# Four single score banks against two double banks in a self attention of a two-layer transformer kernel

## The chip, the cores and the metric

The kernel runs on one core of a Trainium2 chip. The metric is the device time of one execution in microseconds (us), as the median of several runs. Lower is better.

## What is computed

The reference applies two transformer blocks to x of 4 batches x 1024 tokens x 256 channels. Each block is a self attention, a cross attention on a context of 77 tokens and a gated feed forward, each behind a layer norm and with a residual. Block 0 has 16 heads of width 16 and quantised weights; block 1 has 16 heads of width 64. All is float32. The change touches the self attention of block 0 alone:

```python
sim = jnp.einsum('bihd,bjhd->bhij', q, k) * scale
attn = jax.nn.softmax(sim, axis=-1)
out = jnp.einsum('bhij,bjhd->bihd', attn, v).reshape(Bq, Nq, D)
return linear(out, ow, ob)
```

## The kernel before

`attend_narrow` works in 16 **steps**, four for each batch; a step takes a group of four heads. A step has 16 **slots**. The softmax subtracts each query's maximum, so the scores are computed twice: once as queries x keys to find the maximum (line 1501, "scores", reduced by VectorE in line 1369), and once as keys x queries with the maximum already folded into the matmul as extra rows (line 1518, "shifted"), from which ScalarE takes the exponential (line 1481). TensorE multiplies these by the values (line 1530). The first product runs 13 to 16 slots ahead of the second: while step i is in its slots, the maxima of step i+1 (and of the first 3 slots of step i+2) are found. Step 0's maxima, 64 reductions, and 12 of step 1 come before the first slot; at the end, from slot 13 of step 14 on, there are no scores left to do.

The order on TensorE in a slot is written out: the first pair of shifted products (sh0), the scores of key half f = 0, at some slots one **extra**, the scores of f = 1, the second pair of shifted products (sh1), the values of two slots before. A pair is two heads, r = 0 and r = 1, whose matmuls use rows 0 to 63 and 64 to 127 of the array. VectorE takes its work in the same order. TensorE executes in this order and stops at a wait, with all that stands behind it.

The extras are: "back" (slots 2 and 10, four transposes of the output, line 1539, then on VectorE lines 1391 and 1396), "rows" (slot 4 after an odd step, slot 12 of an odd step, line 1547, then ScalarE line 1464 and VectorE line 1404), "turn" (slot 13, the transpose of the maxima, line 1508, then lines 1382 and 1385; VectorE forms the negated maxima just before, line 1373), and "y" (slots 7 and 8 after each fourth step, the output projection, line 1560, then line 1415).

Scores and extras share one ring of PSUM banks, `bank`, in the order in which they come. Every entry of the ring ("unit") has a number u, lies in bank u % 4, and may be written when unit u - 4 has been released: `pe.wait_ge(s_free, u - 3)`, where s_free counts the releases (it starts at RING0 = 4). In a slot with an extra the units are f0 r0, f0 r1, extra, f1 r0, f1 r1 ("y" takes two). The shifted products have a ring of three banks of their own, `stb`, which the exponentials free (p_ready).

```python
for r in range(2):
    u = at["s", i, slot, f, r]
    rows = slice(64 * r, 64 * r + SROWS)
    pe.wait_ge(s_free, u - 3)
    t.matmul(bank[u % 4][:, :], q[cur][rows, j, qb * P:(qb + 1) * P], k_[cur][rows, j, f * HALF:(f + 1) * HALF],
             start=True, stop=True, tile_position=(64 * r, 0)).then_inc(s_ready, 1)
```

Of the kernel before, what the change touches and what calls it, by code (L numbers as in the profile page):

```python
# [5 lines left out]
F32 = mybir.dt.float32  # L6
# [90 lines left out]
class Program:  # L97
# [1125 lines left out]
    def attend_narrow(self, L, x_sb, ident, wo, bo):  # L1223
        nc = self.nc
        QB, KC, HALF, G, HD, W = N // P, N // P, N // 2, L.group, L.hd, L.tile
        SLOTS = 2 * KC
        NP, DEPTH, EARLY, RING0 = 8, 3, 3, 4
        STEPS, NG = L.steps, L.ng
        LAG = 2
        SROWS, TROWS = 3 * HD, 3 * HD + 2  # L1230
# [6 lines left out]

        def scores_of(i, slot):
            for f in range(2):
                for r in range(2):  # L1240
                    unit("s", i, slot, f, r)

        for slot in range(SLOTS):
            scores_of(0, slot)
# [3 lines left out]
        for i in range(STEPS + 1):  # L1248
            for s in range(SLOTS if i < STEPS else 10):
                n, slot = (i + 1, EARLY + s) if s < SLOTS - EARLY else (i + 2, s - SLOTS + EARLY)  # L1250
                for f in range(2):
                    if n < STEPS:
                        unit("s", n, slot, f, 0), unit("s", n, slot, f, 1)
# [12 lines left out]

        with ExitStack() as st:
# [91 lines left out]
            def _(dve):  # L1359
# [2 lines left out]

                def top(i, slot, f):
                    qb, j = slot // 2, slot % 2
                    for r in range(2):
                        u = at["s", i, slot, f, r]
                        dve.wait_ge(s_ready, u + 1)
                        c = ((r * 2 + j) * QB + qb) * 2 + f
                        v.tensor_reduce(mx[:, i % 2, c:c + 1], bank[u % 4][:, :], AX_X, ALU.max).then_inc(s_free, 1)  # L1369

                def negate(i):
                    dve.wait_ge(s_free, at["s", i, SLOTS - 1, 1, 1] + 1)
                    v.tensor_reduce(negm[:, :], mx[:, i % 2, :].rearrange("p (c f) -> p c f", f=2), AX_X, ALU.max,
                                    negate=True).then_inc(negm_done, 1)

                def turned(i):
                    u, par = at["turn", i], i % 2
                    rows = bank[u % 4][0:4 * QB, 0:P]
                    dve.wait_ge(s_ready, u + 1)
                    if i >= 2:  # L1380
                        dve.wait_ge(m_in[(i - 2) % DEPTH], ((i - 2) // DEPTH + 1) * 64)
                    v.tensor_scalar(mm[par][:, 0, :].bitcast(U32), rows.bitcast(U32), HI12, None,
                                    ALU.bitwise_and).then_inc(m_cut, 1)
                    dve.wait_ge(m_cut, i + 1)
                    v.tensor_tensor(mm[par][:, 1, :], rows, mm[par][:, 0, :], ALU.subtract).then_inc(s_free, 1)

                def normalise(n):
                    half, g, u = n % 2, n // 2 % 2, at["back", n // 2, n % 2]
                    view = bank[u % 4][:, :].rearrange("p (b h w) -> p b h w", b=4, w=W)
                    dve.wait_ge(s_ready, u + 1)  # L1390
                    v.reciprocal(rec[:, half, :, :].unsqueeze(3), view[:, :, :, HD:HD + 1]).then_inc(rec_done, 1)
                    dve.wait_ge(rec_done, n + 1)
                    if n >= 4 and g == 0:
                        dve.wait_ge(s_ready, at["rows", n // 2 - 1, half] + 1)
                    out = on[:, half, :, G * HD * g:G * HD * (g + 1)].rearrange("p b (h w) -> p b h w", w=HD)
                    v.tensor_tensor(out, view[:, :, :, 0:HD], rec[:, half, :, :].unsqueeze(3).broadcast_to((P, 4, G, HD)),
                                    ALU.mult).then_inc(s_free, 1)

                def low(n):
# [4 lines left out]
                    v.tensor_tensor(o_lo[:, ch, cols], bank[u % 4][:, :], o_hi[:, ch, cols].bitcast(F32),  # L1404
                                    ALU.subtract).then_inc(s_free, 1)

                def project(i, half):
                    b = i // NG
# [39 lines left out]
            def _(act):  # L1448
# [10 lines left out]
                def high(n):  # L1459
                    half, ch, u = n % 2, n // 4 % 2, at["rows", n // 2, n % 2]  # L1460
                    act.wait_ge(s_ready, u + 1)
                    if n // 2 >= NG:
                        act.wait_ge(s_ready, at["y", (n // 2 // NG) * NG - 1, half, 1] + 1)
                    a_.activation(o_hi[:, ch, half * HALF:(half + 1) * HALF], bank[u % 4][:, :], ACT.Copy).then_inc(hi_done, 1)

                for i in range(STEPS + 1):
                    if i == 1:
# [20 lines left out]
            def _(pe):  # L1488
# [4 lines left out]
                def score(i, slot, f):  # L1493
                    cur, qb, j = i % DEPTH, slot // 2, slot % 2
                    if slot == 0 and f == 0:
                        pe.wait_ge(q_in[cur], (i // DEPTH + 1) * QLOADS)
                    for r in range(2):
                        u = at["s", i, slot, f, r]
                        rows = slice(64 * r, 64 * r + SROWS)
                        pe.wait_ge(s_free, u - 3)  # L1500
                        t.matmul(bank[u % 4][:, :], q[cur][rows, j, qb * P:(qb + 1) * P], k_[cur][rows, j, f * HALF:(f + 1) * HALF],  # L1501
                                 start=True, stop=True, tile_position=(64 * r, 0)).then_inc(s_ready, 1)

                def turn(i):
                    u = at["turn", i]
                    pe.wait_ge(negm_done, i + 1)
                    pe.wait_ge(s_free, u - 3)
                    t.transpose(bank[u % 4][0:4 * QB, 0:P], negm[:, :], ident[:, :]).then_inc(s_ready, 1)

                def shifted(i, s, j):  # L1510
                    cur, half, c = i % DEPTH, s // KC, s % KC
# [22 lines left out]
                def back(n):  # L1534
                    half, u = n % 2, at["back", n // 2, n % 2]
                    pe.wait_ge(o_ready, n + 1)
                    pe.wait_ge(s_free, u - 3)
                    for k in range(4):
                        ins = t.transpose(bank[u % 4][:, k * P:(k + 1) * P], osb[:, half, k * P:(k + 1) * P], ident[:, :])
                    ins.then_inc(s_ready, 1)  # L1540

                def rows(n):
                    half, u = n % 2, at["rows", n // 2, n % 2]
                    pe.wait_ge(s_free, at["back", n // 2, half] + 1)
                    pe.wait_ge(s_free, u - 3)
                    for k in range(4):
                        ins = t.transpose(bank[u % 4][:, k * P:(k + 1) * P], on[:, half, k, :], ident[:, :])
                    ins.then_inc(s_ready, 1)

                def project(i, half):  # L1550
                    pe.wait_ge(s_free, at["rows", i, half] + 1)
                    pe.wait_ge(w_low, 1)
                    for j in range(2):
                        u = at["y", i, half, j]
                        pe.wait_ge(s_free, u - 3)
                        for k in range(2):
                            tok = slice((half * 4 + 2 * j + k) * P, (half * 4 + 2 * j + k + 1) * P)
                            for n, (ch, o, w) in enumerate((ch, o, w) for ch in range(DC)
                                                           for o, w in ((o_hi, w_hi), (o_hi, w_lo), (o_lo, w_hi))):
                                ins = t.matmul(bank[u % 4][:, k * D:(k + 1) * D], o[:, ch, tok], w[:, ch, :],  # L1560
                                               start=n == 0, stop=n == 3 * DC - 1)
                        ins.then_inc(s_ready, 1)

                for slot in range(SLOTS):
                    for f in range(2):
# [1871 lines left out]
```

## Time and profile before

| | |
|---|---|
| median of 3 runs | 4218.95 us (4212.62 to 4226.44) |
| span of the profiled execution, first to last instruction | 4217.9 us |
| TensorE busy over the span | 93% |
| VectorE busy | 66% |
| ScalarE busy | 44% |
| GpSimd busy | 44% |
| first score of this self attention, last value product | 180.7 us, 949 us |
| line 1369, maxima: instructions, mean | 1024, 683 ns |
| line 1481, exponentials: instructions, mean | 1024, 601 ns |
| line 1518, shifted products: instructions, mean | 1024, 472 ns |

PE is TensorE, PEld its weight load, DVE VectorE, ACT ScalarE, POOL GpSimd, SP the queue that issues most DMAs. Line numbers are those of the kernel. "<-" in brackets names what ended the idle time of the engine before an instruction. Matmuls overlap, and the ends of matmuls are modelled, so a busy TensorE need not be at its peak. The profiled execution's own time was not recorded beside its span; the span lies 1.05 us under the median of the three runs.

### The profile page before, as it was taken

What the parts mean: (1) busy time and instruction counts of PE and PEld (TensorE: products, weight loads), DVE (VectorE), ACT (ScalarE), POOL (GpSimd) and SP (SyncE); (2) the same over time, 40 slices, a digit from 0 to 9 for tenths busy, and PEclk for the clock granted to TensorE, in tenths of its full rate; (3) what the DMA queues carried; (4) which work ended last, traced back from release to release, by engine and by line L of the source; (5) the groups of instructions that cost most, each with busy time, mean ns of one, the idle gap of its engine ahead of it and who ended that gap; (6) DMA issues with size and microseconds to landing.
All of it is one profiled execution on the core that took longest, in us unless ns stands there. A gap on an engine that the chain in (4) does not pass through costs nothing. (4 is left out here: it accounts for less than half of the span.)

```text
span 4217.9 us, 64445 instructions
## 1 busy us (share of the span) xinstructions
PE 3909.5 (93%) x24639; PEld 2598.3 (62%) x24639; DVE 2770.9 (66%) x4547; ACT 1839.2 (44%) x2746; POOL 1859.2 (44%) x1203
## 2 busy tenths in 40 slices
PE   3799999994998997998999999999999979999899
PEld 2533443433557886884666666666666647777787
DVE  6599999953536654435676767676766737665665
ACT  1267777771443333442333333333333334444333
POOL 1288970001203002005777777877787753222200
PEclk9789999996779998997999999999999989999899
DMA  4734434405622005883211111121112010000100
GB/s 159 180 56 77 59 57 48 42 2 94 102 43 52 22 13 197 306 308 103 75 51 51 64 63 51 51 76 51 51 51 76 26 31 10 10 10 1 42 15 17
DMA packets 314421, 294.96 MB, mean 70 GB/s; under 512 B 133420, under 2 KB 237292, under 8 KB 313860
## 3 DMA queue, kind: packets, MB, share of 16 engines
q1 hardware_dynamic: 311460, 281.88, 25.7%
q0 software_dynamic: 2656, 8.97, 0.7%
q8 instruction: 197, 3.23, 0.3%
q14 instruction: 108, 0.88, 0.1%
HBM read 161.92 MB, written 127.28 MB: 69 GB/s over the span
## 5 line engine op out<-in xcount | busy, mean ns | idle before, releaser
L1741 POOL TENSOR_TENSOR f_sums<-f_sums,f_probs 128x1024 f32<-128x1024 f32 x384 | 915.5, 2384 | 154.8 <-ACT f_probs L1860 117.1
L1860 ACT ACTIVATE f_probs<-f_st 128x1024 f32<-128x1024 f32 x512 | 525.0, 1027 | 938.7 <-PE f_st L1906 933.9
L1758 DVE TENSOR_REDUCE f_mx<-f_s 128x1 f32<-128x512 f32 x1024 | 659.8, 686 | 380.7 <-PE f_s L1883 369.4
L1369 DVE TENSOR_REDUCE f_mx<-f_s 128x1 f32<-128x512 f32 x1024 | 638.6, 683 | 50.8 <-PE f_s L1501 28.4
L1481 ACT ACTIVATE f_probs<-f_st 128x512 f32<-128x512 f32 x1024 | 535.9, 601 | 225.6 <-PE f_st L1518 225.5
L1883 PE MATMUL f_s<-f_k,f_q 64*128 64x512 f32 x3072 | 515.0, 415 | 18.6 <-DMA f_k<-k 12.5
L1906 PE MATMUL f_st<-f_q,f_k 64*128 64x512 f32 x3072 | 485.2, 390 | 1.1 <-ACT f_probs L1860 1.0
L1920 PE MATMUL f_acc<-f_probs,f_v 128*64 128x512 f32 x2048 | 465.0, 596 | 0.0
L1883 PEld LDWEIGHTS f_s<-f_k,f_q 64*128 64x128 f32 x3072 | 341.2, 189 | 166.6 <-issue 112.1
L1906 PEld LDWEIGHTS f_st<-f_q,f_k 64*128 64x128 f32 x3072 | 366.4, 184 | 25.9 <-ACT f_probs L1860 3.8
L1518 PE MATMUL f_st<-f_q,f_k 50*128 50x512 f32 x1024 | 332.7, 472 | 6.9 <-ACT f_probs L1481 6.8
L588 POOL TENSOR_TENSOR f_ve<-f_var,f_const 128x4 f32<-128x4 f32 x48 | 10.0, 209 | 695.9 <-DVE f_var L569 695.7
L1518 PEld LDWEIGHTS f_st<-f_q,f_k 50*128 50x128 f32 x1024 | 135.8, 185 | 277.5 <-ACT f_probs L1481 263.7
L1920 PEld LDWEIGHTS f_acc<-f_probs,f_v 128*64 128x64 f32 x2048 | 141.3, 137 | 265.9 <-issue 257.0
L1501 PE MATMUL f_s<-f_k,f_q 48*128 48x512 f32 x1024 | 267.3, 455 | 22.5 <-DMA f_k<-k 22.1
L1530 PE MATMUL f_acc<-f_probs,f_v 128*32 128x512 f32 x2048 | 273.0, 606 | 0.0
L1781 DVE RECIPROCAL f_rd<-f_s 128x512 f32<-128x512 f32 x64 | 214.9, 3358 | 72.3 <-PE f_s L1929 72.3
L1906 PE MATMUL f_st<-f_m,f_mones 64*128 64x512 f32 x1024 | 247.8, 389 | 0.0
L3289 ACT ACTIVATE f_gate<-f_pg,f_bias 128x512 f32<-128x512 f32 x128 | 88.0, 688 | 349.1 <-PE f_pg L3335 349.1
L765 DVE TENSOR_TENSOR f_stage<-f_pc,f_stage 128x512 f32<-128x512 f32 x160 | 110.2, 691 | 189.7 <-ACT f_stage L795 189.7
L1737 POOL TENSOR_TENSOR f_sums<-f_probs 128x1024 f32<-128x1024 f32 x64 | 153.3, 2395 | 183.9 <-ACT f_probs L1860 183.9
L3214 DVE SCALAR_TENSOR_TENSOR f_u<-f_pa,f_bias,f_gate 128x512 f32<-128x512 f32 x128 | 96.1, 751 | 202.0 <-PE f_pa L3335 201.9
(320 smaller groups left out, 7874.5 us busy)
## 6 DMA issues: line engine op xcount, KB each, us to landing
q<-f_stage SPq DMA_DIRECT2D x80, 512.0 KB, 2.9
k<-f_stage SPq DMA_DIRECT2D x80, 512.0 KB, 2.9
f_q<-q SPq DMA_DIRECT2D x32, 1024.0 KB, 5.0
f_k<-k SPq DMA_DIRECT2D x32, 1024.0 KB, 7.3
v<-f_v_stage SPq DMA_DIRECT2D x64, 256.0 KB, 3.1
f_v<-v SPq DMA_DIRECT2D x32, 512.0 KB, 8.5
f_q<-q SPq DMA_DIRECT2D x96, 128.0 KB, 4.2
f_k<-k SPq DMA_DIRECT2D x96, 128.0 KB, 6.9
```

The source lines that it names most:

```text
L1369: v.tensor_reduce(mx[:, i % 2, c:c + 1], bank[u % 4][:, :], AX_X, ALU.max).then_inc(s_free, 1)
L1481: a_.activation(probs[:, n % NP, e % 2, :], stb[k % 3][:, :], ACT.Exp, scale=L.scale).then_inc(p_ready, 1)
L1501: t.matmul(bank[u % 4][:, :], q[cur][rows, j, qb * P:(qb + 1) * P], k_[cur][rows, j, f * HALF:(f + 1) * HALF], start=True, stop=True, tile ...
L1518: t.matmul(stb[n % 3][:, :], k_[cur][rows, j, c * P:(c + 1) * P], q[cur][rows, j, half * HALF:(half + 1) * HALF], start=True, stop=True, t ...
L1530: ins = t.matmul(acc[W * h:W * h + W, :], vs[cur][:, c, h, :], p, start=c == 0, stop=c == KC - 1, tile_position=(0, W * h))
L1741: g_.tensor_tensor(out, out, probs[:, n % NP, :, :], ALU.add).then_inc(sum_done, 1)
L1758: v.tensor_reduce(mx[:, i % 2, c:c + 1], bank[u % 3][:, :], AX_X, ALU.max).then_inc(s_free, 1)
L1781: v.reciprocal(rd[:, half, :], bank[u % 3][:, :]).then_inc(s_free, 1)
L1860: a_.activation(probs[:, s % NP, :, :], stb[s % 2][:, :, :], ACT.Exp, scale=L.scale).then_inc(p_ready, 1)
L1883: ins = t.matmul(bank[u % 3][:, :], q[cur][rows, a, qb * P:(qb + 1) * P], k_[cur][rows, c, f * HALF:(f + 1) * HALF], start=r == 0, stop=r ...
L1906: ins = t.matmul(stb[s % 2][:, h, :], lhs, rhs, start=r == 0, stop=r == 3, tile_position=(64 * h, 0))
L1920: ins = t.matmul(acc[W * h:W * h + W, :], vs[cur][:, c, h, :], probs[:, s % NP, h, :], start=c == 0, stop=c == KC - 1, tile_position=(0, W ...
```

## The change

The ring becomes two banks of double size. One unit now holds both heads of a pair, its release is one count, and one VectorE instruction takes both maxima. Extras take a whole double bank each and use half of it; "y" uses both halves as one unit, with one addition of 1024 columns instead of two of 512. A unit u may be written when unit u - 2 has been released. The layout of `mx` follows.

```diff
-        NP, DEPTH, EARLY, RING0 = 8, 3, 3, 4
+        NP, DEPTH, EARLY, RING0 = 8, 3, 3, 2
...
             for f in range(2):
-                for r in range(2):
-                    unit("s", i, slot, f, r)
+                unit("s", i, slot, f)
...
-                        unit("y", i - 1, s - 7, 0), unit("y", i - 1, s - 7, 1)
+                        unit("y", i - 1, s - 7)
...
-            mx = sb("mx", [P, 2, 4 * QB * 2])
+            mx = sb("mx", [P, 2, 2, 2 * QB * 2])
...
-            bank = [ps(f"s{k}", [P, 512]) for k in range(4)]
+            bank = [ps(f"s{k}", [P, 2, 512]) for k in range(2)]
...
-                    for r in range(2):
-                        u = at["s", i, slot, f, r]
-                        dve.wait_ge(s_ready, u + 1)
-                        c = ((r * 2 + j) * QB + qb) * 2 + f
-                        v.tensor_reduce(mx[:, i % 2, c:c + 1], bank[u % 4][:, :], AX_X, ALU.max).then_inc(s_free, 1)
+                    u, c = at["s", i, slot, f], (j * QB + qb) * 2 + f
+                    dve.wait_ge(s_ready, u + 1)
+                    v.tensor_reduce(mx[:, i % 2, :, c], bank[u % 2][:, :, :], AX_X, ALU.max).then_inc(s_free, 1)
...
-                    for j in range(2):
-                        u = at["y", i, half, j]
-                        k = b * QB + half * 4 + 2 * j
-                        xt = x_sb[:, k:k + 2, :]
-                        dve.wait_ge(biased, b + 1)
-                        dve.wait_ge(s_ready, u + 1)
-                        v.tensor_tensor(xt, xt, bank[u % 4][:, :].rearrange("p (t d) -> p t d", d=D),
-                                        ALU.add).then_inc(s_free, 1)
+                    b, u = i // NG, at["y", i, half]
+                    k = b * QB + half * 4
+                    xt = x_sb[:, k:k + 4, :]
+                    dve.wait_ge(biased, b + 1)
+                    dve.wait_ge(s_ready, u + 1)
+                    v.tensor_tensor(xt, xt, bank[u % 2][:, :, :].rearrange("p j (t d) -> p (j t) d", d=D),
+                                    ALU.add).then_inc(s_free, 1)
...
+                    u = at["s", i, slot, f]
+                    pe.wait_ge(s_free, u - 1)
                     for r in range(2):
-                        u = at["s", i, slot, f, r]
                         rows = slice(64 * r, 64 * r + SROWS)
-                        pe.wait_ge(s_free, u - 3)
-                        t.matmul(bank[u % 4][:, :], q[cur][rows, j, qb * P:(qb + 1) * P], k_[cur][rows, j, f * HALF:(f + 1) * HALF],
-                                 start=True, stop=True, tile_position=(64 * r, 0)).then_inc(s_ready, 1)
+                        ins = t.matmul(bank[u % 2][:, r, :], q[cur][rows, j, qb * P:(qb + 1) * P],
+                                       k_[cur][rows, j, f * HALF:(f + 1) * HALF], start=True, stop=True, tile_position=(64 * r, 0))
+                    ins.then_inc(s_ready, 1)
```

The turn, back and rows transposes and their readers change in the same way: `bank[u % 4]` becomes `bank[u % 2]` (its first half), and `u - 3` becomes `u - 1`.

## Rows read from the trace of the kernel before

**Rows 1.** Busy time of each engine in a steady stretch of the stage; "x" counts instructions.

```profile
core 0: us, PE busy (x) PEld busy (x) DVE busy (x) ACT busy (x) POOL busy (x), PEclk, DMA share, GB/s
360.00:857.00 497.00, 492.25 (x3072) 202.62 (x3071) 467.14 (x797) 380.60 (x729) 233.04 (x93) 1.00 0.41 53
```

**Rows 2.** Timeline of one plain slot and the next one's start: start, length, instructions.

```profile
519.92 0.50 PE L1518 MATMUL f_st<-f_q,f_k 50*128 50x512 f32 x2
520.26 0.86 PE L1501 MATMUL f_s<-f_k,f_q 48*128 48x512 f32 x4
520.46 2.07 ACT L1481 ACTIVATE f_probs<-f_st 128x512 f32<-128x512 f32 x4 [0.54 <-PE f_st L1518]
520.63 0.18 PEld L1501 LDWEIGHTS f_s<-f_k,f_q 48*128 48x128 f32 x1 [0.18 <-DVE f_mx L1369]
...
521.10 0.18 PEld L1518 LDWEIGHTS f_st<-f_q,f_k 50*128 50x128 f32 x1 [0.29 <-ACT f_probs L1481]
...
521.53 1.06 PE L1530 MATMUL f_acc<-f_probs,f_v 128*32 128x512 f32 x8
...
522.53 0.50 PE L1518 MATMUL f_st<-f_q,f_k 50*128 50x512 f32 x2
```

**Rows 3.** Timeline of a slot of the last step, which has no scores.

```profile
916.30 0.73 PE L1518 MATMUL f_st<-f_q,f_k 50*128 50x512 f32 x3
916.83 2.07 ACT L1481 ACTIVATE f_probs<-f_st 128x512 f32<-128x512 f32 x4 [0.54 <-PE f_st L1518]
917.48 0.18 PEld L1518 LDWEIGHTS f_st<-f_q,f_k 50*128 50x128 f32 x1 [0.89 <-ACT f_probs L1481]
...
917.90 1.06 PE L1530 MATMUL f_acc<-f_probs,f_v 128*32 128x512 f32 x8
918.90 0.29 PEld L1518 LDWEIGHTS f_st<-f_q,f_k 50*128 50x128 f32 x3 [0.84 <-ACT f_probs L1481]
```

**Rows 4.** VectorE's opening, and reductions of 512 and of 2048 columns elsewhere.

```profile
181.52 38.36 DVE L1369 TENSOR_REDUCE f_mx<-f_s 128x1 f32<-128x512 f32 x64 [22.24 <-PE f_s L1501]
```

```profile
L288 DVE TENSOR_REDUCE f_ext<-f_w 128x1 f32<-128x512 f32 x6 | 4.1, 678 | 3.2 <-DMA f_w<-L_xattn_q_w 2.7 <-DMA f_w<-L_xattn_v_w 0.5
...
L288 DVE TENSOR_REDUCE f_ext<-f_w 128x1 f32<-128x2048 f32 x1 | 2.3, 2276 | 0.0
```

**Rows 5.** Timeline of a slot with a "back".

```profile
525.13 0.50 PE L1518 MATMUL f_st<-f_q,f_k 50*128 50x512 f32 x2
...
525.91 0.69 DVE L1369 TENSOR_REDUCE f_mx<-f_s 128x1 f32<-128x512 f32 x1
...
526.51 0.65 PE L1501 MATMUL f_s<-f_k,f_q 48*128 48x512 f32 x2
...
528.32 0.50 PE L1518 MATMUL f_st<-f_q,f_k 50*128 50x512 f32 x2
```

**Rows 6.** Timeline of a "y" slot, from its second pair of scores to the next slot.

```profile
427.20 0.49 PE L1501 MATMUL f_s<-f_k,f_q 48*128 48x512 f32 x2
...
428.86 0.50 PE L1518 MATMUL f_st<-f_q,f_k 50*128 50x512 f32 x2
```

**Rows 7.** Timeline, TensorE: start and end of a "rows" slot, and of two "turn" slots.

```profile
508.94 0.50 PE L1518 MATMUL f_st<-f_q,f_k 50*128 50x512 f32 x2
...
512.11 0.50 PE L1518 MATMUL f_st<-f_q,f_k 50*128 50x512 f32 x2
...
533.53 0.50 PE L1518 MATMUL f_st<-f_q,f_k 50*128 50x512 f32 x2
...
536.76 0.50 PE L1518 MATMUL f_st<-f_q,f_k 50*128 50x512 f32 x2
```

```profile
489.32 0.50 PE L1518 MATMUL f_st<-f_q,f_k 50*128 50x512 f32 x2
...
492.73 0.50 PE L1518 MATMUL f_st<-f_q,f_k 50*128 50x512 f32 x2
```

**Rows 8.** Two stretches around the rise of TensorE's clock (PEclk, the share granted).

```profile
210.00:220.00 10.00, 8.34 (x14) 3.74 (x14) 9.96 (x18) 0.00 (x0) 9.99 (x5) 0.50 0.00 0
236.40:240.00 3.60, 3.60 (x27) 1.68 (x23) 2.65 (x5) 2.46 (x5) 3.46 (x2) 1.00 1.77 62
```

More of the change, by code:

```diff
@@ L1252, in attend_narrow @@
                     if n < STEPS:
-                        unit("s", n, slot, f, 0), unit("s", n, slot, f, 1)
+                        unit("s", n, slot, f)
                     if f == 0 and s == SLOTS - EARLY and i + 1 < STEPS:
@@ L1364, in top @@
                     qb, j = slot // 2, slot % 2
[L1365 to L1369 removed]
+                    u, c = at["s", i, slot, f], (j * QB + qb) * 2 + f
+                    dve.wait_ge(s_ready, u + 1)
+                    v.tensor_reduce(mx[:, i % 2, :, c], bank[u % 2][:, :, :], AX_X, ALU.max).then_inc(s_free, 1)
                 def negate(i):
[L1372 to L1373 removed]
+                    dve.wait_ge(s_free, at["s", i, SLOTS - 1, 1] + 1)
+                    v.tensor_reduce(negm[:, :], mx[:, i % 2, :, :].rearrange("p r (c f) -> p (r c) f", f=2), AX_X, ALU.max,
                                     negate=True).then_inc(negm_done, 1)
@@ L1377, in turned @@
                     u, par = at["turn", i], i % 2
-                    rows = bank[u % 4][0:4 * QB, 0:P]
+                    rows = bank[u % 2][0:4 * QB, 0, 0:P]
                     dve.wait_ge(s_ready, u + 1)
@@ L1388, in normalise @@
                     half, g, u = n % 2, n // 2 % 2, at["back", n // 2, n % 2]
-                    view = bank[u % 4][:, :].rearrange("p (b h w) -> p b h w", b=4, w=W)
+                    view = bank[u % 2][:, 0, :].rearrange("p (b h w) -> p b h w", b=4, w=W)
                     dve.wait_ge(s_ready, u + 1)
@@ L1403, in low @@
                     dve.wait_ge(hi_done, k + 1)
-                    v.tensor_tensor(o_lo[:, ch, cols], bank[u % 4][:, :], o_hi[:, ch, cols].bitcast(F32),
+                    v.tensor_tensor(o_lo[:, ch, cols], bank[u % 2][:, 0, :], o_hi[:, ch, cols].bitcast(F32),
                                     ALU.subtract).then_inc(s_free, 1)
                 def project(i, half):
-                    b = i // NG
-                    for j in range(2):
-                        u = at["y", i, half, j]
-                        k = b * QB + half * 4 + 2 * j
-                        xt = x_sb[:, k:k + 2, :]
-                        dve.wait_ge(biased, b + 1)
-                        dve.wait_ge(s_ready, u + 1)
-                        v.tensor_tensor(xt, xt, bank[u % 4][:, :].rearrange("p (t d) -> p t d", d=D),
-                                        ALU.add).then_inc(s_free, 1)
+                    b, u = i // NG, at["y", i, half]
[5 more added lines that the diff above has]
+                                    ALU.add).then_inc(s_free, 1)
                 for slot in range(SLOTS):
@@ L1462, in high @@
                     if n // 2 >= NG:
-                        act.wait_ge(s_ready, at["y", (n // 2 // NG) * NG - 1, half, 1] + 1)
-                    a_.activation(o_hi[:, ch, half * HALF:(half + 1) * HALF], bank[u % 4][:, :], ACT.Copy).then_inc(hi_done, 1)
+                        act.wait_ge(s_ready, at["y", (n // 2 // NG) * NG - 1, half] + 1)
+                    a_.activation(o_hi[:, ch, half * HALF:(half + 1) * HALF], bank[u % 2][:, 0, :], ACT.Copy).then_inc(hi_done, 1)
                 for i in range(STEPS + 1):
@@ L1506, in turn @@
                     pe.wait_ge(negm_done, i + 1)
-                    pe.wait_ge(s_free, u - 3)
-                    t.transpose(bank[u % 4][0:4 * QB, 0:P], negm[:, :], ident[:, :]).then_inc(s_ready, 1)
+                    pe.wait_ge(s_free, u - 1)
+                    t.transpose(bank[u % 2][0:4 * QB, 0, 0:P], negm[:, :], ident[:, :]).then_inc(s_ready, 1)
                 def shifted(i, s, j):
@@ L1536, in back @@
                     pe.wait_ge(o_ready, n + 1)
-                    pe.wait_ge(s_free, u - 3)
+                    pe.wait_ge(s_free, u - 1)
                     for k in range(4):
-                        ins = t.transpose(bank[u % 4][:, k * P:(k + 1) * P], osb[:, half, k * P:(k + 1) * P], ident[:, :])
+                        ins = t.transpose(bank[u % 2][:, 0, k * P:(k + 1) * P], osb[:, half, k * P:(k + 1) * P], ident[:, :])
                     ins.then_inc(s_ready, 1)
@@ L1544, in rows @@
                     pe.wait_ge(s_free, at["back", n // 2, half] + 1)
-                    pe.wait_ge(s_free, u - 3)
+                    pe.wait_ge(s_free, u - 1)
                     for k in range(4):
-                        ins = t.transpose(bank[u % 4][:, k * P:(k + 1) * P], on[:, half, k, :], ident[:, :])
+                        ins = t.transpose(bank[u % 2][:, 0, k * P:(k + 1) * P], on[:, half, k, :], ident[:, :])
                     ins.then_inc(s_ready, 1)
@@ L1552, in project @@
                     pe.wait_ge(w_low, 1)
[L1553 to L1562, printed above, removed]
+                    u = at["y", i, half]
+                    pe.wait_ge(s_free, u - 1)
+                    for k in range(4):
+                        tok = slice((half * 4 + k) * P, (half * 4 + k + 1) * P)
+                        for n, (ch, o, w) in enumerate((ch, o, w) for ch in range(DC)
+                                                       for o, w in ((o_hi, w_hi), (o_hi, w_lo), (o_lo, w_hi))):
+                            ins = t.matmul(bank[u % 2][:, k // 2, k % 2 * D:(k % 2 + 1) * D], o[:, ch, tok], w[:, ch, :],
+                                           start=n == 0, stop=n == 3 * DC - 1)
+                    ins.then_inc(s_ready, 1)
                 for slot in range(SLOTS):
```

## The prediction

> **What bounds the kernel now.** The page comes first, to find the stage: the edit touches the 770 us of the first self attention and nothing behind it, so only that stretch is read. Second comes the table of busy time over a steady part of it [rows 1]: of 497 us TensorE is busy 492 and VectorE 467, or 94%. That reads as if VectorE's maxima set the pace, and the timeline of a plain slot seems to confirm it [rows 2]: TensorE's slot starts at 519.92 and the next at 522.53, 2.61 us apart, a second weight load at 520.63 waits for a maximum, and four maxima of 683 ns lie in it. Third, and against it, comes a slot of the last step [rows 3], which has no scores and so no maxima at all. It lasts from 916.30 to 918.90, 2.60 us. The slot is as long without VectorE's work as with it, so VectorE does not set it.
>
> What does is a circle between TensorE and ScalarE. The first exponential starts 0.54 after the slot; the second matmul of sh1 waits for it, since the ring of shifted products has three banks, and goes 1.18 after the slot's start, both with scores (521.10) and without (917.48); the values follow 0.43 later and hold TensorE for 1.00, and then the next slot starts: 1.18 + 0.43 + 1.00 = 2.61 [rows 2, 3]. The scores fit into TensorE's wait for ScalarE. I hold this circle for the bound of the plain slots.
>
> **The cost of the new maximum.** Before, 64 maxima in a row took 38.36 us [rows 4]. The last one's recorded length is 0.68, so they start (38.36 - 0.68) / 63 = 0.598 us apart, although each is recorded at 0.683. A reduction of 2048 columns took 2276 ns against 678 for 512, so a column costs 1598 / 1536 = 1.04 ns [rows 4], and 512 more columns 0.533 us. A maximum over both banks should thus last 0.683 + 0.533 = 1.216, and such maxima should start 0.598 + 0.533 = 1.131 apart, where two single ones took 1.196. That is 0.065 per pair. No row shows a reduction with the new pair form. The dearest bound is no saving at all: a length of 2 x 0.683 = 1.37, 0.15 more than I take. Cheaper than 1.04 ns a column no row suggests. I take 1.216, since two rows of one kind of instruction give the slope.
>
> The Trainium skill bears on this from two sides ("Perfetto Trace Analysis", section Optimizing Scalar/DVE Operations). It gives about 125 ns of overhead for each VectorE instruction on PSUM and says that larger operations help if the engine is saturated; with 512 instructions fewer that would be an estimate of 64 us gained if VectorE were the bound. In the same place it says that if VectorE isn't saturated but causes bubbles on other engines, breaking instructions up may let work complete sooner. This change does the reverse of the latter. The rows above speak for the second case.
>
> **Plain slots: nothing.** Pair f0 would be ready when its first half is now, and VectorE starts it 0.78 after the slot's start (525.91 - 525.13, where VectorE is idle too) [rows 5]. Two pairs take 2 x 1.131 = 2.26, so the f1 pair is recorded as done at 0.78 + 1.131 + 1.216 = 3.13, which is 0.52 after the next slot's start. The f1 scores there start around 0.6 now, and anything up to about 0.9 leaves sh1's second matmul at 1.18. What covers the change is the wait for ScalarE; were it gone, TensorE would be held by the maxima at 2.26 a slot. At the dear bound the f1 pair is done at 3.43, or 0.82 in: still covered, barely. Plain slots cost 0.
>
> **Slots with an extra: about half a microsecond each.** This is where the change bites. Before, the units of such a slot are f0 r0, f0 r1, extra, f1 r0, f1 r1; with four banks f1 r0 needs the release of a unit of the slot before, and f1 r1 that of f0 r0, which is one short maximum. Now the units are f0, extra, f1 in two banks: f1 must wait until the whole f0 pair of the same slot is reduced, since the extra has taken the other bank. It goes at 0.78 + 1.216 + 0.05 = 2.05, the 0.05 being the step from a recorded end on VectorE to the start that it releases: the f0 r0 maximum ends at 525.91 + 0.69 = 526.60, and the second matmul of the pair started there goes at 526.51 + 0.65 - 0.50 = 526.66. Before, the first of that pair went at 526.51, or 1.38 [rows 5]. Behind it on TensorE stand sh1, the values and the next slot; all engines wait for these. How far the next slot is from an f1 pair that goes late with nothing left to wait for, the "y" slot shows: 427.20 to 428.86, 1.66 us [rows 6]. So each slot with one extra becomes 2.05 + 1.66 = 3.71 long. VectorE's work on the extra falls behind f0 as before, and its f1 maximum then ends 0.1 to 0.3 into the next slot, which is early enough; nothing is given back later, because the next slot is again bound by the circle.
>
> Now the kinds, with their lengths before:
> - "back", 528.32 - 525.13 = 3.19 [rows 5]: +0.52. With scores beside it there are 29 (slot 10 of steps 0 to 14, slot 2 of 1 to 14): 15.1 us.
> - "rows", 512.11 - 508.94 = 3.17 [rows 7]: +0.54. 7 at slot 4 and 7 at slot 12: 7.6 us.
> - "turn", 536.76 - 533.53 = 3.23, and behind a "rows" slot, in odd steps, 492.73 - 489.32 = 3.41 [rows 7]: +0.48 and +0.30, 7 of each up to step 13: 3.4 + 2.1 = 5.5 us. The negated maxima are not later than now, so the DMAs of the maxima go out on time.
> - "y", 6 with scores beside them: here TensorE's 24 matmuls of the projection are longer than the f0 maximum, so f1 doesn't wait for it. But the one addition of 1024 columns starts only when all 24 are done, the f1 maximum stands behind it, and the second "y" must wait for that: I work out -0.1, +0.25 and +0.1 for the two slots and the next, 0.2 for each of 3 pairs: 0.7 us.
>
> Sum: +28.9 us. Not covered by anything, since in each of these slots TensorE is the one that waits.
>
> **The opening: a small gain.** There VectorE is the bound: 38 pairs of maxima come before the first slot, each 0.065 shorter, -2.5 us [rows 4]. TensorE's clock is at half (1.2 GHz) there and goes to full (2.4 GHz) by 236.4, 10 us into the slots [rows 8]. In the new form the scores of the opening come as two matmuls side by side with longer rests between. If the rise came some slots later, it would cost a few us; I see no row that decides it and take 0.
>
> Total: 4217.9 + 28.9 - 2.5 = 4244.3 for the profiled span, which lies 1.05 below the median of the runs: **4245 us**, 0.6% slower.
>
> **The rivals.** About 0.3% (12.7 us) is what a measurement of this kernel can tell from no change.
> 1. VectorE sets the slots after all, and the change is faster. Place: the plain slots. In the busy view 4 maxima fill 2.60. The price would be 512 x 0.065 = 33 us off, and more if the merged rows are taken at their word; against it stand slots of 2.60 with no maxima [rows 3]. It decides only if the circle with ScalarE is shorter than 2.6 while scores run, and the wait of an extra slot is covered too. Time 4219 - 33 = 4186. Chance 0.06. The Trainium skill's rule on saturation, named above, would come out here.
> 2. The extra slots' wait is hidden. For it: TensorE's weight loads wait 0.84 for ScalarE in every slot [rows 3]; against it: those are waits of the loader while value products stream. Only the opening's gain would be left: 4216, same. If half is hidden, 4230. Chance of landing within 0.3%: 0.14.
> 3. The pair maximum is dearer than two single ones. From a distance of 1.30 between starts on, two of them outlast 2.61 and VectorE sets the plain slots. At 1.45, 0.32 more than I take, 174 plain slots with scores (15 x 16 - 3 - 57 - 6) grow by 0.29, the 57 extra ones by 0.32 and the opening's 38 pairs by 0.32: 4245 + 50 + 18 + 12 = 4325. Nothing in the rows speaks for it. Chance 0.04.
>
> **How the numbers follow.** The forecast has 0.76. Its own range: at the dear bound of the maximum the 57 extra slots with scores (without "y") grow by 0.15 more, 8.6, and the opening gains nothing, 2.5: 4256; a clock that rises late adds up to 5: 4261. Downwards, if a quarter of the waits is covered, 4238. To leave out no more than 2 in 10 the range reaches to the half-hidden case and some run-to-run shift: 4226 to 4262. Slower 0.80, same 0.14, faster 0.06.
>
> **What would show it.** After the change: line 1369 with 512 maxima near 1.22 us; plain slots still 2.60 to 2.61; slots with an extra 3.6 to 3.8 instead of 3.2, with the weight load of the scores waiting 0.5 or more for a maximum; VectorE less busy; the first slot some 2 us earlier. Plain slots shorter than 2.5 would make me wrong about the bound; extra slots unchanged at 3.2 wrong about the wait; plain slots longer wrong about the price.

## The result, and the profile after

| | before | after |
|---|---|---|
| median of 5 runs each | 4215.95 us (4212.49 to 4226.44) | 4247.23 us (4246.51 to 4255.88) |
| ratio, 95% interval | | 1.0065 [1.0045, 1.0086] |
| span of the profiled execution | 4217.9 | 4244.3 |
| maxima: instructions, mean | 1024, 683 ns | 512, 1221 ns |

The change makes the kernel 0.65% slower. Line numbers shift by a few: scores are now line 1496, maxima 1366, shifted products 1514, values 1526, exponentials 1476, "back" 1535.

The steady stretch, busy time by engine, the same 497 us as in [rows 1]:

```profile
360.00:857.00 497.00, 463.43 (x2942) 180.87 (x2942) 427.41 (x422) 364.07 (x697) 228.90 (x91) 1.00 0.39 52
```

Every engine is less busy than in [rows 1], VectorE 427 us instead of 467, and TensorE gets 2942 matmuls done where it was 3072, 4.2% fewer. No engine has taken over as the bound. All of them wait more.

A plain slot, which answers to [rows 2]:

```profile
548.88 0.50 PE L1514 MATMUL f_st<-f_q,f_k 50*128 50x512 f32 x2
549.22 0.63 PE L1496 MATMUL f_s<-f_k,f_q 48*128 48x512 f32 x4
...
549.66 2.36 DVE L1366 TENSOR_REDUCE f_mx<-f_s 128x2 f32<-128x1024 f32 x2 [0.67 <-PE f_s L1496]
549.69 0.88 PE L1514 MATMUL f_st<-f_q,f_k 50*128 50x512 f32 x2
550.07 0.18 PEld L1514 LDWEIGHTS f_st<-f_q,f_k 50*128 50x128 f32 x1 [0.43 <-ACT f_probs L1476]
...
550.50 1.06 PE L1526 MATMUL f_acc<-f_probs,f_v 128*32 128x512 f32 x8
...
551.49 0.50 PE L1514 MATMUL f_st<-f_q,f_k 50*128 50x512 f32 x2
```

It lasts 551.49 - 548.88 = 2.61 as before. VectorE is done with its two maxima 0.53 into the next slot. It idles 0.67 before this slot's scores, since a "turn" slot stands in front of it, and 0.24 to 0.26 in the plain slots that follow; in the stretch of [rows 1] it was idle for 6% of the time. The weight load that stops TensorE is still that of sh1's second matmul, at 1.19 into the slot, and it waits for ScalarE.

A slot with a "back", which answers to [rows 5]:

```profile
559.31 0.50 PE L1514 MATMUL f_st<-f_q,f_k 50*128 50x512 f32 x2
...
560.10 1.23 DVE L1366 TENSOR_REDUCE f_mx<-f_s 128x2 f32<-128x1024 f32 x1 [0.25 <-PE f_s L1496]
...
560.10 0.66 PE L1535 MATMUL f_s<-ident,f_osb 128*128 128x128 f32 x4
...
561.38 0.50 PE L1496 MATMUL f_s<-f_k,f_q 48*128 48x512 f32 x2 [0.62 <-DVE f_mx L1366]
...
561.72 0.40 PE L1514 MATMUL f_st<-f_q,f_k 50*128 50x512 f32 x2
...
562.05 1.07 PE L1526 MATMUL f_acc<-f_probs,f_v 128*32 128x512 f32 x8
...
563.04 0.50 PE L1514 MATMUL f_st<-f_q,f_k 50*128 50x512 f32 x2
```

The pair's maximum starts 0.79 into the slot and lasts 1.23; the f1 scores start 0.05 after its end, 2.07 into the slot; the next slot comes 1.66 later, at 3.73. TensorE's matmuls stand still for 0.62 us with the maximum named as the releaser, which [rows 5] do not have.

The waits of the stage (230 to 905 us), as total, times and longest: the changed kernel, then the one before.

```profile
PEld f_s L1496 <- DVE f_mx L1366: 89.2, 172, 1.3
...
PE f_s L1496 <- DVE f_mx L1366: 42.5, 59, 1.1
```

```profile
PEld f_s L1501 <- DVE f_mx L1369: 32.6, 169, 0.4
```

The wait of scores for a maximum grows from 32.6 to 131.7 us. The loader (PEld) can wait while matmuls are still running, so the row to read here is the second, the matmuls' own waits: 59 of them, 42.5 us, where the list of the kernel before has no such row at all. Even this row is not the loss: the slots grew by 30.0 us (next table), and in a later experiment the same loss comes with 5.9 us in it.

All 255 slot lengths, from one start of sh0 to the next, added up by kind (us, in brackets the mean); "again" is a second profile of the same kernel, below. "Plain" includes three slots of step 14 that have no scores:

```
                    count  before         again          after          again
start of 1st slot          226.4          224.6          224.5          224.4
first four slots       4    12.7           14.3           13.2           13.1
plain                173   451.2 (2.61)   452.8 (2.62)   451.1 (2.61)   451.1 (2.61)
back                  29    92.2 (3.18)    92.2 (3.18)   108.0 (3.72)   108.0 (3.72)
rows                  14    44.5 (3.18)    44.5 (3.18)    52.0 (3.72)    52.1 (3.72)
turn, even steps       7    22.5 (3.22)    22.5 (3.21)    26.1 (3.72)    26.1 (3.72)
turn, odd steps        7    23.9 (3.42)    23.9 (3.42)    26.0 (3.72)    26.1 (3.72)
y                      6    32.3 (5.39)    32.3 (5.39)    33.3 (5.55)    33.3 (5.55)
last step             15    39.5 (2.63)    39.5 (2.63)    42.2 (2.81)    46.9 (3.12)
all behind it             3272.7         3260.8         3268.0         3265.2
span                      4217.9         4207.4         4244.3         4246.2
```

The slots with an extra and scores grow by 15.8 + 7.5 + 3.6 + 2.1 + 1.0 = 30.0 us, and these kinds agree between two profiles of a kernel to 0.1. The other lines are another matter. In the repeat of the kernel before, TensorE's clock stayed at half until 244.5 us instead of 236.3, which covers the fourth slot (4.06) and the first plain ones (4.07 and 2.91); so the first four and the plain slots come out 1.6 longer each in sum. Behind the last step two executions of the same kernel differ by 12 us. Sums can be off by 0.1 by rounding.

### The profile page after: what moved, and what is told of

Read it like the earlier page. It is cut to its first block and busy times, and to the rows that moved or that the text cites. A ratio compares the mean times of both kernels' runs of the same rounds, so it can differ in the third digit from the quotient of the medians.

```text
span 4244.3 us, 63917 instructions
## 1 busy us (share of the span) xinstructions
PE 3884.1 (92%) x24639; PEld 2566.6 (60%) x24639; DVE 2736.7 (64%) x4027; ACT 1839.5 (43%) x2746; POOL 1858.8 (44%) x1203
## 5 line engine op out<-in xcount | busy, mean ns | idle before, releaser
L1753 DVE TENSOR_REDUCE f_mx<-f_s 128x1 f32<-128x512 f32 x1024 | 659.4, 686 | 380.7 <-PE f_s L1878 369.4
L1366 DVE TENSOR_REDUCE f_mx<-f_s 128x2 f32<-128x1024 f32 x512 | 607.0, 1221 | 102.2 <-PE f_s L1496 100.6
L1878 PE MATMUL f_s<-f_k,f_q 64*128 64x512 f32 x3072 | 515.2, 414 | 18.6 <-DMA f_k<-k 12.4
L1514 PE MATMUL f_st<-f_q,f_k 50*128 50x512 f32 x1024 | 305.9, 470 | 6.8 <-ACT f_probs L1476 6.6
L1496 PE MATMUL f_s<-f_k,f_q 48*128 48x512 f32 x1024 | 213.5, 463 | 78.1 <-DVE f_mx L1366 55.7
```

The costliest lines, as they stand in the source:

```text
L1366: v.tensor_reduce(mx[:, i % 2, :, c], bank[u % 2][:, :, :], AX_X, ALU.max).then_inc(s_free, 1)
L1496: ins = t.matmul(bank[u % 2][:, r, :], q[cur][rows, j, qb * P:(qb + 1) * P], k_[cur][rows, j, f * HALF:(f + 1) * HALF], start=True, stop=T ...
L1514: t.matmul(stb[n % 3][:, :], k_[cur][rows, j, c * P:(c + 1) * P], q[cur][rows, j, half * HALF:(half + 1) * HALF], start=True, stop=True, t ...
L1753: v.tensor_reduce(mx[:, i % 2, c:c + 1], bank[u % 3][:, :], AX_X, ALU.max).then_inc(s_free, 1)
L1878: ins = t.matmul(bank[u % 3][:, :], q[cur][rows, a, qb * P:(qb + 1) * P], k_[cur][rows, c, f * HALF:(f + 1) * HALF], start=r == 0, stop=r ...
```

## The experiments

The theory: plain slots are set by the circle of TensorE and ScalarE, and a slot with an extra now waits for the whole pair of the same slot, since the ring has two places and the extra takes one. Rivals: the long reduction as such does it; the extras are longer for another reason than the ring; VectorE is the bound after all and the circle a coincidence.

**Two single maxima in the double bank.** The ring stays at two units, the instruction goes back to the short form; the release comes with the second.

```diff
-                    v.tensor_reduce(mx[:, i % 2, :, c], bank[u % 2][:, :, :], AX_X, ALU.max).then_inc(s_free, 1)
+                    v.tensor_reduce(mx[:, i % 2, 0, c:c + 1], bank[u % 2][:, 0, :], AX_X, ALU.max)
+                    v.tensor_reduce(mx[:, i % 2, 1, c:c + 1], bank[u % 2][:, 1, :], AX_X, ALU.max).then_inc(s_free, 1)
```

> The two double banks stay, but a unit is reduced by two single maxima, and only the second releases it. If the ring is what costs (my theory), a slot with an extra has its f1 scores at 0.78 + 0.60 + 0.68 + 0.05 = 2.11 and is 3.77 us long against 3.72 in the changed kernel, 57 of these give +3 us, and the opening's 2.5 us are lost again: a span near 4250 us, ratio to the kernel before about 1.008. If the long maximum instruction itself is what costs (rival), this kernel is back within 4 us of the kernel before, near 4220.

Median 4264.13, ratio to before 1.0123 [1.0089, 1.0157], span 4250.5. TensorE in a slot with a "back":

```profile
562.43 0.50 PE L1515 MATMUL f_st<-f_q,f_k 50*128 50x512 f32 x2
...
564.56 0.50 PE L1497 MATMUL f_s<-f_k,f_q 48*128 48x512 f32 x2 [0.68 <-DVE f_mx L1367]
...
566.22 0.50 PE L1515 MATMUL f_st<-f_q,f_k 50*128 50x512 f32 x2
```

The slot lasts 3.79, with f1 at 2.13 and again 1.66 behind it. Plain slots stay at 2.61. So the instruction isn't what costs: with the old instruction and the new ring the extra slots are longer still, by 0.07, about what the pair form saves. The long reduction as the cause falls. The span came as expected (4250). The median did not: the profiled run was the fastest of four, and the highest was 4276.66. What made the others slower no trace shows.

**The kernel before, with extras that take two places.** Here the instruction and the banks stay as they were; "turn", "back" and "rows" take two units of the ring of four.

```diff
-            order.append(key)
+            order.extend([key] * (2 if key[0] in ("turn", "back", "rows") else 1))
...
-                    pe.wait_ge(s_free, u - 3)
+                    pe.wait_ge(s_free, u - 2)
...
-                                    ALU.mult).then_inc(s_free, 1)
+                                    ALU.mult).then_inc(s_free, 2)
```

> The kernel before, with its four single banks and single maxima, in which a back, rows or turn takes two places of the ring instead of one. If it is the place that the extra takes away (my theory), the second f1 score waits for the second f0 maximum, goes 2.11 into the slot, and the slots with an extra are about 3.75 long instead of 3.2, 57 of them: +31 us, a span near 4249. Plain slots stay 2.61. If the cost comes only from releasing both banks of a pair with one instruction (rival), this kernel stays near 4218, and the slots with an extra near 3.2.

Median 4254.04, ratio 1.0083 [1.0055, 1.0111], span 4252.1. TensorE in a "back" slot:

```profile
564.11 0.50 PE L1518 MATMUL f_st<-f_q,f_k 50*128 50x512 f32 x2
...
565.63 1.10 PE L1501 MATMUL f_s<-f_k,f_q 48*128 48x512 f32 x2
566.23 0.73 PE L1518 MATMUL f_st<-f_q,f_k 50*128 50x512 f32 x2
...
567.89 0.50 PE L1518 MATMUL f_st<-f_q,f_k 50*128 50x512 f32 x2
```

"Back" and "rows" slots are 3.77 long, plain ones 2.61, and "y", which took two places already, 5.39 as before. "Turn" slots are 3.78 to 3.80, and up to 4.66 where the clock fell. The one thing changed in this kernel is that such an extra takes half of the ring instead of a quarter, and that alone gives the loss of the change in all these kinds; only the 1.0 us of "y" is not in it. That one instruction releases both banks of a pair is not needed for the loss. The share of the ring that an extra takes is the cause, shown from both sides.

The list of waits hides it here. The matmuls' own waits for a maximum are 5.9 us over the stage against 42.5 in the changed kernel, although the slots are as long: the two matmuls of f1 run one behind the other (1.10 us for both instead of 0.50), so TensorE counts as busy while the pair is held up. Slot lengths show the loss in both kernels, the list in one.

**Exponentials cut to a quarter, in both kernels.** This shortens ScalarE's part of the circle, to see which engine sets the plain slot. The kernels leave out three quarters of the probabilities; GpSimd fills these once with 1.0 ahead of the stage, and TensorE does the same matmuls over them. The same edit in both:

```diff
-                                a_.activation(probs[:, n % NP, e % 2, :], stb[k % 3][:, :], ACT.Exp, scale=L.scale).then_inc(p_ready, 1)
+                                a_.activation(probs[:, n % NP, e % 2, 0:128], stb[k % 3][:, 0:128], ACT.Exp, scale=L.scale).then_inc(p_ready, 1)
```

> The kernel before, with each exponential of this attention taken over 128 of its 512 columns (the other three quarters of the probabilities are left out). An exponential then lasts about 0.28 instead of 0.60. Theory: the circle shrinks to 0.54 + 0.28 + 0.05 + 0.43 + 1.00 = 2.30, below VectorE's 4 x 0.598 = 2.39, so the plain slots become 2.39 to 2.42, bound by the maxima. Rival (the maxima set them at 2.60 now): the plain slots stay at 2.60.

> The changed kernel with the same cut of the exponentials to 128 of 512 columns. Theory: VectorE needs only 2 x 1.14 = 2.28 for a slot, so the circle of 2.30 shows, and the plain slots are 2.30 long, 0.1 less than in the other kernel with the same cut: only here is the cheaper maximum worth something. The slots with an extra stay near 3.7, since they wait for the f0 maximum and not for ScalarE. Rival: plain slots equal in both.

Spans 4176.4 and 4216.0 (one run each). Slots of the last step, which has no scores, go from 2.60 to 2.28 in both. Plain slots with scores go to 2.47 on average in the kernel before (2.39 to 2.42 was expected), and to 2.41 in the changed one (2.30 was expected); TensorE of the latter:

```profile
327.16 0.50 PE L1515 MATMUL f_st<-f_q,f_k 50*128 50x512 f32 x2
...
329.45 0.50 PE L1515 MATMUL f_st<-f_q,f_k 50*128 50x512 f32 x2
...
330.35 0.50 PE L1497 MATMUL f_s<-f_k,f_q 48*128 48x512 f32 x2 [0.17 <-DVE f_mx L1367]
...
332.01 0.50 PE L1515 MATMUL f_st<-f_q,f_k 50*128 50x512 f32 x2
```

A slot of 2.29 alternates with one of 2.56 that waits for a maximum. That is the circle: take ScalarE's time away and the slot shrinks though VectorE does what it did, and only then do the maxima come to the surface. In that state the pair maximum is worth 0.06 a plain slot, less than the 0.1 that I expected and half of what two pairs save back to back (2 x 0.065). It isn't enough: 170 x 0.06 = 10 us, against 31 in the extra slots, which are 3.72 again. The changed kernel's last slot starts 18.6 us later even here. Of the 39.6 us between the spans, the other 21.0 lie behind the stage, where the program is the same, so they say nothing of the change.

**Four banks for the shifted products, three for the scores.** The kernel before, with the circle opened by a fourth bank; the ring of scores pays for it, and the order becomes sh0, sh1, f0, values, extra, f1. ScalarE's copy for "rows" moves behind the four exponentials of its slot.

```diff
-            bank = [ps(f"s{k}", [P, 512]) for k in range(4)]
-            stb = [ps(f"st{k}", [P, 512]) for k in range(3)]
+            bank = [ps(f"s{k}", [P, 512]) for k in range(3)]
+            stb = [ps(f"st{k}", [P, 512]) for k in range(4)]
```

> From the kernel before: the shifted products get four banks, the scores and extras three, and TensorE's order in a slot becomes sh0, sh1, f0, values, extra, f1. Theory (the circle of shifted products, exponentials and values through three banks sets the plain slots at 2.61): the circle is opened, and VectorE's maxima set them at 4 x 0.598 = 2.39 to 2.45, so 174 plain slots give 28 to 38 us and the slots with an extra some more; the turn comes later and may cost 5 us. Span 4170 to 4195, ratio 0.989 to 0.995. Rival (VectorE already sets the plain slots): they stay at 2.6 or grow with the smaller ring, ratio 1.00 or above.

Median 4241.75, ratio 1.0054 [1.0034, 1.0074], span 4239.7: a miss by about 45 us. Half of it holds. TensorE in the last step:

```profile
963.63 1.18 PE L1518 MATMUL f_st<-f_q,f_k 50*128 50x512 f32 x4
964.74 1.06 PE L1530 MATMUL f_acc<-f_probs,f_v 128*32 128x512 f32 x8
965.74 1.04 PE L1518 MATMUL f_st<-f_q,f_k 50*128 50x512 f32 x4
966.71 1.07 PE L1530 MATMUL f_acc<-f_probs,f_v 128*32 128x512 f32 x8
```

Here slots without scores last 1.97 and 2.11 in turn where they were 2.60, and 2.17 on average over the last step (2.63 before). In these slots the order on TensorE is the old one, so three banks are what closes the circle. But with scores most plain slots are 2.69 to 2.71 long, those behind a "back" 2.90, and the weight loads of one say why:

```profile
577.06 0.18 PEld L1501 LDWEIGHTS f_s<-f_k,f_q 48*128 48x128 f32 x1 [0.51 <-DVE f_mx L1369]
```

The second matmul of f0 now waits for a maximum. I had counted what three score banks leave to VectorE and not that f0 must wait for the f1 of the slot before, which goes behind the values. The rival's forecast (2.6 or more, ratio 1.00 or above) came true, by the smaller ring that it names; that VectorE sets the old plain slots is not shown by it, since this kernel changes ring and order as well. The kernel's eight banks (scores, shifted products, one for the values) stay eight: each ring wants the one that the other has.

**The extras behind the values.** The changed kernel, with "back" and "rows" at the slot's end, so that f0, f1 and the extra alternate in two banks with longer between them (ScalarE's line 1459, 1464 before, follows):

```diff
-                            if f == 0 and s == 2 and i > 0:
-                                back(2 * i - 1)
-                            if f == 0 and s == 4 and i > 0 and (i - 1) % 2 == 1:
-                                rows(2 * i - 1)
...
+                        if s == 2 and i > 0:
+                            back(2 * i - 1)
+                        if s == 4 and i > 0 and (i - 1) % 2 == 1:
+                            rows(2 * i - 1)
```

> The changed kernel with back and rows moved behind the values, to the end of their slots (turn and y stay). Theory: the unit that the extra then waits for was released long before, f1 goes at 0.6, and a back slot is 2.61 + 0.5 = 3.1 long instead of 3.72: 29 x 0.6 = 18 us less. A rows slot gains less, since ScalarE now takes its rows behind the four exponentials and delays the next ones by 0.3: 14 x 0.3 = 4 us less. Span near 4222, ratio to the kernel before 1.000 to 1.002. Rival (the pair maximum slows something else): it stays above 4238.

Median 4251.96, ratio 1.0082 [1.0051, 1.0112], span 4242.3: a miss by 20 us, and above the 4238 that the rival named, though not by its reason. The extra slots themselves get shorter, "back" to 3.28 (3.1 was expected) and "rows" to 3.19. The wait went elsewhere. TensorE in and behind a "rows" slot:

```profile
522.78 0.66 PE L1543 MATMUL f_s<-ident,f_on 128*128 128x128 f32 x4
523.36 0.50 PE L1514 MATMUL f_st<-f_q,f_k 50*128 50x512 f32 x2
...
524.85 0.50 PE L1496 MATMUL f_s<-f_k,f_q 48*128 48x512 f32 x2 [0.74 <-DVE f_o_lo L1401]
...
526.50 0.50 PE L1514 MATMUL f_st<-f_q,f_k 50*128 50x512 f32 x2
```

The bank of "rows" is freed by VectorE's line 1401, which waits for ScalarE's copy; f1 of the next slot waits for that, and this slot lasts 526.50 - 523.36 = 3.14 instead of 2.61. Where the next slot is a "turn", it lasts 4.41 instead of 3.72. And TensorE's clock was at half for 37.5 us of the stage in this run, which lengthened "turn" slots to up to 5.76 and plain ones to 4.07; that is roughly 13 us of the miss (an estimate: what the plain and "turn" slots have over their lengths at full clock).

**Only "back" behind the values.** The same edit without "rows":

```diff
-                            if f == 0 and s == 2 and i > 0:
-                                back(2 * i - 1)
...
+                        if s == 2 and i > 0:
+                            back(2 * i - 1)
```

> The changed kernel with only back moved to the end of its slots; rows stays where it was, so that ScalarE and the turn behind it are not disturbed. Its 29 slots should be 3.28 long, as in the kernel with both moved, instead of 3.72: 12.8 us less, a span near 4231 if TensorE's clock stays up in the stage, ratio to the kernel before about 1.003. Rival: whatever is taken from the waits of the extras is lost again to falls of the clock, and the span stays near 4242.

Median 4238.1, ratio 1.0043 [1.0025, 1.0062], span 4239.5. TensorE in a "back" slot:

```profile
552.59 0.50 PE L1514 MATMUL f_st<-f_q,f_k 50*128 50x512 f32 x2
...
555.29 0.66 PE L1535 MATMUL f_s<-ident,f_osb 128*128 128x128 f32 x4
555.87 0.49 PE L1514 MATMUL f_st<-f_q,f_k 50*128 50x512 f32 x2
```

3.28 instead of 3.72, in 29 slots 12.8 us less, as expected, and the kinds beside it unchanged. The span was expected near 4231 if the clock stayed up, and it did not: the last step took 55.3 us, 13.1 more than in the changed kernel's first profile (last section). It is the best form of the new ring that I found, 10.6 us under the changed kernel's median on the same chip, and still slower than the kernel before: "rows", "turn" and "y" remain.

**Both kernels once more.** Unchanged, beside the last one, on its chip.

> The changed kernel once more, unaltered, beside the kernel before on the same chip. The plain and extra slots should repeat to 0.01 us (2.61 and 3.72). What I don't know is whether TensorE's clock falls again in the last step of this attention (2.7 us lost there in the first profile), and whether the cross attention behind it again takes 7.7 us less than before. If these come from the kernel they repeat; if they are chance, the span moves by up to 5 us either way from 4244. Ratio 1.005 to 1.009.

> The kernel before once more, unaltered, for the same question: slots 2.61 and 3.18, and a cross attention of about 216 us if its clock pattern belongs to the kernel, anything from 205 to 220 if it is chance. Span 4213 to 4223.

The changed kernel: median 4248.66, ratio 1.0076 [1.0054, 1.0099], span 4246.2. The kernel before: one run, 4209.57, span 4207.4, under the 4213 that I had as the least. Their slots are in the table above. The clock fell again in the last step of the changed kernel, for longer. The cross attention took 208.8 us, as in its first profile (208.6). In the kernel before it took 201.8, below even the 205 to 220 for chance.

## Why the prediction was right, point by point

**The bound.** Plain slots stayed at 2.61 though the maxima got cheaper. The short exponentials took them to 2.47 in the kernel before with the same maxima, and the short exponentials and the fourth bank both shortened the slots without scores. That 94% of VectorE was not the bound is thus shown, not only read off [rows 1 to 3].

**The maximum's price.** 1.216 was forecast, 1.221 is the mean. Starts 1.131 apart: the opening shows 32 of them.

```profile
181.45 36.29 DVE L1366 TENSOR_REDUCE f_mx<-f_s 128x2 f32<-128x1024 f32 x32 [22.52 <-PE f_s L1496]
```

(36.29 - 1.22) / 31 = 1.131, and 2.07 us less than [rows 4] for 32 pairs, 0.065 each. The Trainium skill's 125 ns for each VectorE instruction on PSUM ("Perfetto Trace Analysis", section Optimizing Scalar/DVE Operations) is twice what merging saves here; no run here shows why. Its other sentence, on breaking instructions up where they cause bubbles on another engine, points to the right engine and not to the cause. Broken up again in the double bank, the maxima left the extra slots at 3.79, and four single releases with extras of two places left them at 3.77.

**The extra slots.** 2.05 + 1.66 = 3.71 was forecast; 2.07 + 1.66 = 3.73 is in the rows above, 3.72 the mean of all. By kind, forecast and measured: "back" 15.1 and 15.8, "rows" 7.6 and 7.5, "turn" 5.5 and 5.7.

**"y".** 0.7 was forecast, 1.0 came. (The three parts of the forecast, -0.1, +0.25 and +0.1, make 0.25 for each pair, not 0.2.) The mechanism was that the one addition of 1024 columns delays f1's maximum:

```profile
434.05 1.22 DVE L1410 TENSOR_TENSOR x_rows<-x_rows,f_s 128x1024 f32<-128x1024 f32 x1 [1.90 <-PE f_s L1555]
```

The second "y" slot of the pair then has to wait for that maximum:

```profile
436.55 0.36 PE L1555 MATMUL f_s<-f_w_hi,f_o_hi 128*128 128x256 f32 x1 [0.28 <-DVE f_mx L1366]
```

All of it falls on the second slot of each pair, 5.72 instead of 5.39 (0.33), and none on the first or the next, where I had put -0.1 and +0.1.

**The opening.** Forecast -2.5, measured -1.9 for the first slot's start. The repeat of the kernel before starts at 224.6 too, without any change, so these 2 us are within what its own start varies by; the maxima's part is sure (2.07), its arrival at the end is not. The first four slots took 0.5 more. The clock rose at 235.6 us in the changed kernel, against 236.3 before, so the later rise that I had feared did not come; 244.5 in the repeat of the kernel before shows that this moment moves without any change.

**The sum.** The profiled span came to the forecast 4244.3 exactly, and that is partly luck. Of the growth, +30.0 - 1.9 + 0.5 - 0.1 = +28.5 had to do with the terms of the sum, which made 26.4. Two parts that no term had are of opposite sign: +2.7 in the last step, where the clock fell (last section), and -4.8 behind it, where TensorE has the same work. By the slots the terms were thus 2.1 us too small. Measured by medians, the difference is 31.3 and, in the repeat beside the kernel before, 29.6 us; the first has an interval of about 19 to 36 us, which holds 26.4. The forecast was right by its steps, to 0.7 us for each kind of slot; to the last microsecond it was right by chance.

**The rivals.** VectorE as the bound (4186) and a dearer maximum (4325) fall by the rows above. That the wait is hidden (4216, or 4230 by half) falls too: no part of the 0.54 was covered.

## What to carry to other kernels

The number of units in a ring of buffers counts, beside its bytes. Four small units and two double ones hold the same, but a rare user that takes "one unit" takes a quarter of the first and half of the second. TensorE then waits for the whole first pair of the same slot, and not only for its first half. Before merging instructions on an engine that looks 94% busy, look for a stretch where its work is absent: if the period is the same there, the saving is worth nothing in the regular slots, and only the coarser ring is left. Cost the irregular slots one by one; here 173 of 240 slots did not change, and the others decided.

## What the runs showed that I had not expected

**The clock fell in the last step of the changed kernel.** Three stretches of it, columns as in [rows 1] (the third from last is the granted clock):

```profile
925.00:958.00 33.00, 27.86 (x161) 8.56 (x161) 3.33 (x7) 26.79 (x52) 0.00 (x0) 1.00 0.01 1
958.00:966.10 8.10, 7.64 (x30) 2.26 (x31) 0.68 (x2) 4.83 (x9) 0.00 (x0) 0.58 0.00 1
966.10:976.00 9.90, 8.84 (x52) 2.96 (x52) 0.69 (x1) 8.40 (x17) 0.00 (x0) 1.00 0.00 0
```

For 6.8 us TensorE ran at 1.2 GHz instead of 2.4. The slots there were 3.58 and 4.42 long; TensorE, from one to the next:

```profile
957.83 0.73 PE L1514 MATMUL f_st<-f_q,f_k 50*128 50x512 f32 x3
959.01 0.60 PE L1514 MATMUL f_st<-f_q,f_k 50*128 50x512 f32 x1 [0.46 <-ACT f_probs L1476]
959.55 1.93 PE L1526 MATMUL f_acc<-f_probs,f_v 128*32 128x512 f32 x8
961.41 0.79 PE L1514 MATMUL f_st<-f_q,f_k 50*128 50x512 f32 x2
```

The values hold TensorE for 1.93 instead of 1.06. The kernel before does the same work in its last step, in its first profile

```profile
906.00:945.00 39.00, 33.31 (x192) 10.58 (x189) 2.06 (x5) 32.51 (x63) 0.00 (x0) 1.00 0.00 1
```

with TensorE 85% busy against 84% in the changed kernel before the fall, and keeps its clock. The longest time that TensorE stood idle in the last step is 0.46 us in both, up to the fall in the changed kernel. The repeat of the changed kernel was at half for 20.5 us there, and the kernel with only "back" moved for 41, so that its last step took 55.3 us instead of 39.5:

```profile
949.00:969.00 20.00, 18.96 (x63) 5.14 (x62) 0.00 (x0) 10.73 (x21) 0.00 (x0) 0.50 0.01 1
```

```profile
924.00:965.00 41.00, 38.57 (x125) 10.68 (x125) 0.68 (x2) 21.38 (x42) 0.00 (x0) 0.50 0.00 1
```

Over the whole stage behind the opening, the clock was at half for 0 and 0 us in the two profiles of the kernel before, and for 6.8, 20.5, 20.5, 34.1, 37.5, 13.7 and 41.0 us in the seven other full kernels (the changed one, its repeat, two single maxima, two places, extras last, four banks, back last); with the short exponentials for 0 in both. What sets it off is open. More waits on TensorE would be a guess, and one number speaks against it: the changed kernel with short exponentials has the same long extra slots and no fall. No run took the waits of the last step apart.

**A stretch that no one touched differs by 14.5 us between executions of the same kernel.** A stretch of the cross attention, between the same two matmuls; the kernel before, its repeat, and the changed kernel:

```profile
1056.30:1272.60 216.30, 200.91 (x1215) 119.38 (x1215) 98.37 (x212) 103.41 (x132) 27.42 (x36) 0.79 0.44 71
```

```profile
1059.20:1261.00 201.80, 186.60 (x1215) 110.36 (x1215) 98.05 (x212) 103.18 (x132) 27.41 (x36) 0.85 0.47 75
```

```profile
1091.50:1300.10 208.60, 197.93 (x1215) 117.14 (x1215) 95.13 (x212) 103.56 (x132) 27.36 (x36) 0.79 0.45 73
```

The instructions are the same 1215, the shortest comes with the higher mean clock. So one profile against another can't resolve 10 us over a whole kernel of this kind. The lengths of slots by kind can, where the clock is up: the extra kinds repeat to 0.1 us in sum. Medians over several runs give the rest.
